# Two heads in one out projection: the halves of each head's outputs added by VectorE

## The chip, the cores and the metric

The kernel runs on one core of a Trainium2 chip. The metric is the device time of one execution in microseconds (us), and what counts is the median of several runs.

## What is computed

The program is one block of a network over 2048 rows of 128 channels: a mixture of eight experts, an RWKV layer, the mixture again, a small gated layer with integer weights, attention with 16 heads, and the gated layer again. The change is in the attention:

```python
xn = rms_norm(x, gamma)                       # 2048 x 128
q, k, v = split(xn @ w_qkv)                   # 16 heads of 64 columns
sim = einsum('bhid,bhjd->bhij', q * 64 ** -0.5, k)
attn = softmax(sim)
out = einsum('bhij,bhjd->bhid', attn, v)
x = x + concat_heads(out) @ w_out             # 1024 x 128
```

All of it is in float32. The kernel keeps this accuracy with products of a high and a low part: a value is rounded to the type that TensorE multiplies fast (high), what is left is a second number (low), and high x high, high x low and low x high are added.

## The kernel before

Channels lie on the partitions, rows on the free axis. The engines run programs of their own and meet at semaphores. In the attention stage every engine goes through the heads in order, two heads (even and odd) to a pair. A head has four chunks `c` of 512 queries, a chunk has eight groups `g` of two tiles of 128 keys. `main_chunk` stands once in the program of TensorE (line 930), of ScalarE (1258) and of VectorE (1619), with one `for g` loop each; `window` does it for GpSimd and for SyncE, which issues all DMAs. The order inside a group is written out by hand.

For each group TensorE forms transposed scores (`scores_t`, lines 879 and 880, four matmuls of 512 columns), then two matmuls of scores for the next head's maxima (`score_pair`, line 857), then the values of the group three before (`values`, PV_LAG = 3, lines 894 and 897). ScalarE makes exp twice, into `p_raw` (line 1253) and rounded into `p_h` (1256). GpSimd subtracts the two into `p_l` (line 608, four buffers: it waits until the values of four groups before are done). VectorE takes the maxima of the next head's scores (line 1580) and sums `p_raw` for the softmax's denominators: four pieces `first_half_sum` in groups 4 to 7 (line 1560), four pieces `whole_sum` in groups 0 to 3 of the next chunk (line 1574), each ahead of the group's maximum. `score_pair` waits for the maximum before it, since all of them use banks 4 and 5 of PSUM.

The values of a chunk gather in one bank of PSUM, 6 or 7 in turn. The weights of one values matmul hold the high and the low part of v side by side, so rows 0 to 63 of the bank become the sum with v's high part (p's high and low parts) and rows 64 to 127 the sum with v's low part. The two halves are not added: in group 2 of the next chunk (COPY_GROUP) ScalarE copies all 128 rows into `o_raw` (`copy_out`, line 1242), and the out projection adds them, because `w_o` holds the head's 64 rows of `w_out` twice (`load_o`, line 432).

The other of the two banks is the spare bank. The list SPARE says what TensorE does in it in which group: v and q, k projections for later heads, the turn of the maxima, the column sums of the denominators (line 906, group 4 or 5) and the out projection (line 913, group 7 or 6). The first of a chunk waits for `o_done`, since the bank held the sums of the chunk before; each later one waits until the one before it has been taken out (`evicted`).

The denominators go ScalarE, memory, VectorE, memory (`store_sums`, `load_sums`, `invert`, `store_inverse`, `load_inverse`) and come back two chunks later as `r_bc`, the reciprocals on all 128 partitions. GpSimd multiplies `o_raw` with it in group 3 (`scale`, line 631), TensorE projects, and VectorE adds the result to x in group 0 of the chunk after that, or in group 7 of the last (`add_out`, line 1598).

The last head has no next head, so no maxima, and it doesn't use the plan. For it TensorE spreads the sums over all partitions (`end_sums`, line 1008), VectorE inverts 512 columns out of PSUM (`end_invert`, 1605), multiplies `o_raw` (`end_scale`, 1612), TensorE projects (`end_out`, 1015) and VectorE adds (`end_add`, 1617); the plan for chunk c of it deals with chunk c - 1.

Of the kernel before, what the change touches and what calls it, by code (L numbers as in the profile page):

```python
# [5 lines left out]
fp32 = mybir.dt.float32  # L6
fp32r = mybir.dt.float32r
# [27 lines left out]
PV_LAG = 3  # L35
PRIME = 1
# [26 lines left out]
END_SUMS, END_INVERT, END_SCALE, END_OUT = 4, 5, 6, 7  # L63
END_TURN, END_LATE_OUT, END_LATE_ADD = 3, 5, 6
# [21 lines left out]
def macaron_kernel(nc, a, out, g_scratch, l_scratch, r_scratch):  # L86
    ctx = ExitStack()
    with ctx:
# [76 lines left out]
        p_l = sb("p_l", [128, 4, 2, CH], fp32r, two)  # L165
# [83 lines left out]
        end_l, end_r, end_o, end_ps = sem("end_l"), sem("end_r"), sem("end_o"), sem("end_ps")  # L249
# [42 lines left out]
        def spare_plan(head, c, par, project, has_next):  # L292

            plan = []
            for at, kind, n in SPARE[c]:
# [10 lines left out]
                if kind == "out" and not exists(before(head, c, 2)[0]):  # L306
                    continue
# [3 lines left out]
        def wait_x(eng, k, c):  # L311
# [5 lines left out]
            elif k == 1 or k == 3:  # L317
                eng.wait_ge(y_add, E * ((k // 2) * NC + c + 1))
            else:
                eng.wait_ge(x_ready, PRIME + NC * (k - 4) + c + 1)  # L320
# [13 lines left out]
        def _(sp):  # L334
# [58 lines left out]
            def store_sums(head, c):  # L393
                sp.wait_ge(l_done, chunk_of(head, c) + 1)
                sp.dma_start(l_scratch[ds(head, 1), chunk(c)], l_row[:, :]).then_inc(l_stored, 16)
# [36 lines left out]
            def load_o(head, par):  # L432

                for rows in (slice(0, DH), slice(DH, 128)):
                    sp.dma_start(w_o[par][rows, :], a["w_out"][ds(head * DH, DH), :]).then_inc(wo_loaded, 16)

            def window(pair, par, project, late_project, qk_after, v_after):
# [3 lines left out]
                for c in range(NC):  # L441
# [4 lines left out]
                    if exists(scaled[0]) and not (last and c > 0):  # L446
# [7 lines left out]
                    if c == 2 and not last:  # L454
# [6 lines left out]
                        if not (isinstance(head, int) and head == 0):  # L461
                            sp.wait_ge(out_ps, NC * head)
                        load_o(head + 1, 1 - par)
# [3 lines left out]
                    if exists(summed[0]) and not last:  # L467
# [10 lines left out]
            load_o(0, 0)  # L478
# [21 lines left out]
            window(PAIRS - 1, 1, False, False, False, False)  # L500
# [1239 lines left out]
```

## Time and profile before

| | us |
|---|---|
| median of three runs | 2123.63 |
| lowest and highest | 2120.82, 2125.29 |
| the profiled execution, whole | 2122.15 |
| its span in the trace | 2120.2 |
| attention from the first exp of head 0 to the last add | 600.5 to 2071.9 |

| engine | busy in the span |
|---|---|
| TensorE (PE) | 1998.7 us, 94% |
| VectorE (DVE) | 1773.6 us, 84% |
| GpSimd (POOL) | 1548.2 us, 73% |
| ScalarE (ACT) | 1458.5 us, 69% |

Matmuls are pipelined and overlap in the records, so a busy PE isn't PE at its peak. In a timeline, a number in brackets at the end of a row is the idle time of the engine ahead of it, with what ended that; a row without one followed the row ahead of it at once. `xn` is the tile that holds `o_raw` and `r_bc`.

### The profile page before, as it was taken

How to read it: one execution, taken by the hardware profiler on the slowest of the kernel's cores; microseconds unless marked ns; L12 is line 12 of the kernel's file. 1: busy time of each engine (PE TensorE's matmuls, PEld its weight loads, DVE VectorE, ACT ScalarE, POOL GpSimd, SP SyncE). 2: the span in 40 equal slices, each digit the busy share in tenths (PEclk: the TensorE clock that was granted, in tenths of full speed). 3: DMA queues.
4: the chain of work that ended last, by engine and by line, in shares of the span. 5: the costliest groups of instructions: out<-in, count | busy, mean ns of one | idle time of the engine just before them, and what ended most of it. 6: DMA issues, size and time to landing. Idle time of an engine off the chain costs nothing. (4 is left out here: it accounts for less than half of the span.)

```text
span 2120.2 us, 25547 instructions
## 1 busy us (share of the span) xinstructions
PE 1998.7 (94%) x8290; PEld 1423.8 (67%) x8290; DVE 1773.6 (84%) x1964; ACT 1458.5 (69%) x1800; POOL 1548.2 (73%) x767
## 2 busy tenths in 40 slices
PE   7999999998689999999999999999999999999867
PEld 5777777776457667666766766676676767666545
DVE  5677777655678998998999899899989989999885
ACT  4555455444257887887888787787878878787754
POOL 4332233232068999899899899999989999999862
PEclk9999999997789999999999999999999999999987
DMA  6111211300502230312213031231313213030000
GB/s 185 51 31 41 41 25 17 70 26 1 123 0 40 50 73 13 71 33 57 55 37 70 14 75 38 47 69 24 70 19 70 54 39 70 12 75 12 6 0 20
DMA packets 78942, 96.77 MB, mean 46 GB/s; under 512 B 32055, under 2 KB 35559, under 8 KB 78431
## 3 DMA queue, kind: packets, MB, share of 16 engines
q1 hardware_dynamic: 78814, 95.15, 20.5%
q8 instruction: 70, 1.15, 0.2%
q14 instruction: 58, 0.48, 0.1%
HBM read 43.19 MB, written 1.42 MB: 21 GB/s over the span
## 5 line engine op out<-in xcount | busy, mean ns | idle before, releaser
L608 POOL TENSOR_TENSOR p_l<-p_raw,p_h 128x1024 fp32r<-128x1024 f32 x512 | 1241.4, 2455 | 147.8 <-ACT p_h L1256 132.6
L1253 ACT ACTIVATE p_raw<-ps 128x1024 f32<-128x1024 f32 x512 | 567.2, 1108 | 242.8 <-PE ps L880 241.9
L1580 DVE TENSOR_REDUCE m_part<-ps 128x1 f32<-128x1024 f32 x480 | 584.5, 1218 | 125.7 <-PE ps L857 124.8
L1256 ACT ACTIVATE p_h<-ps 128x1024 fp32r<-128x1024 f32 x512 | 523.8, 1023 | 0.0
L879 PE MATMUL ps<-qa,ka 128*128 128x512 f32 x1024 | 445.8, 435 | 2.0 <-ACT m_t L1224 2.0
L880 PE MATMUL ps<-qb,kb 65*128 65x512 f32 x1024 | 409.2, 400 | 0.0
L894 PE MATMUL ps<-p_h,v_hl 128*128 128x512 f32 x1024 | 403.0, 394 | 1.0 <-POOL p_l L608 0.6
L1574 DVE TENSOR_REDUCE l_sum<-p_raw 128x128 f32<-128x1280 f32 x256 | 377.0, 1476 | 0.4
L857 PE MATMUL ps<-ka,qa 128*128 128x512 f32 x960 | 314.9, 409 | 11.9 <-DVE m_part L1580 11.8
L897 PE MATMUL ps<-p_l,v_hl 128*64 128x512 f32 x1024 | 321.6, 395 | 0.0
L1560 DVE TENSOR_REDUCE p_raw<-p_raw 128x128 f32<-128x1024 f32 x256 | 308.9, 1208 | 12.7 <-ACT p_raw L1253 12.7
L548 POOL TENSOR_TENSOR x<-x,y_gated 128x512 f32<-128x512 f32 x64 | 89.1, 1393 | 261.8 <-DVE y_gated L1448 261.7
L879 PEld LDWEIGHTS ps<-qa,ka 128*128 128x128 f32 x1024 | 195.1, 191 | 113.7 <-issue 73.3
L1439 DVE SCALAR_TENSOR_TENSOR h_l<-ps,h_h 128x512 fp32r<-128x512 f32 x256 | 176.0, 688 | 112.7 <-ACT h_h L1159 110.5
L1159 ACT ACTIVATE h_h<-ps 128x512 fp32r<-128x512 f32 x256 | 150.3, 594 | 168.5 <-PE ps L704 167.8
L894 PEld LDWEIGHTS ps<-p_h,v_hl 128*128 128x128 f32 x1024 | 193.7, 189 | 77.6 <-issue 3.3
L857 PEld LDWEIGHTS ps<-ka,qa 128*128 128x128 f32 x960 | 172.1, 190 | 90.6 <-DVE m_part L1580 57.6
L880 PEld LDWEIGHTS ps<-qb,kb 65*128 65x128 f32 x1024 | 195.2, 191 | 53.6 <-issue 16.4
L897 PEld LDWEIGHTS ps<-p_l,v_hl 128*64 128x64 f32 x1024 | 138.6, 135 | 71.7 <-issue 1.5
L702 PE MATMUL ps<-x_h,w_l 128*128 128x512 f32 x256 | 118.2, 462 | 4.6 <-DVE h_l L1439 2.5
L703 PE MATMUL ps<-x_h,w_h 128*128 128x512 f32 x256 | 102.5, 400 | 0.0
L704 PE MATMUL ps<-x_l,w_h 128*128 128x512 f32 x256 | 102.3, 400 | 0.0
(206 smaller groups left out, 2406.4 us busy)
## 6 DMA issues: line engine op xcount, KB each, us to landing
g_bc<-g_scratch SPq DMA_DIRECT2D x64, 256.0 KB, 5.2
xn<-r_scratch SPq DMA_DIRECT2D x59, 256.0 KB, 4.1
qa<-qk_hi SPq DMA_DIRECT2D x112, 128.0 KB, 2.4
ka<-qk_hi SPq DMA_DIRECT2D x56, 128.0 KB, 2.4
kb<-qk_hi SPq DMA_DIRECT2D x56, 128.0 KB, 2.4
ka<-xn SPq DMA_DIRECT2D x28, 128.0 KB, 2.3
qb<-xn SPq DMA_DIRECT2D x28, 128.0 KB, 2.3
ka<-qk_low SPq DMA_DIRECT2D x28, 128.0 KB, 3.7
```

Of the source, the lines that this page charges most:

```text
L608: nc.gpsimd.tensor_tensor(p_l[:, g % 4, :, :], slots(g), p_h[:, g % 4, :, :].bitcast(fp32), ALU.subtract).then_inc(pl_done, 1)
L857: last = mm(ps[:, 4 + b, :], qa[par][:, it * 128:it * 128 + 128], ka[par][:, chunk(2 * half + b)], start=True, stop=True)
L879: mm(st, ka[par][:, jt * 128:jt * 128 + 128], qa[par][:, ds(c * CH, CH)], start=True, stop=False)
L880: last = mm(st, kb[par][:, jt * 128:jt * 128 + 128], qb[par][:, ds(c * CH, CH)], start=False, stop=True)
L894: return mm(ps[:, bank, :], v_hl[:, par, 2 * g + j, :], p_h[:, g % 4, j, :], start=start, stop=stop)
L897: return mm(ps[0:DH, bank, :], v_hl[:, par, 2 * g + j, 0:DH], p_l[:, g % 4, j, :], start=False, stop=False)
L1253: af(slots(g), s_t, ACT.Exp).then_inc(raw_done, 1)
L1256: af(p_h[:, g % 4, :, :], s_t, ACT.Exp).then_inc(ph_done, 1)
L1439: stt(h_l[:, t % 4, :], ps[:, t % 4, :], 0.0, h_h[:, t % 4, :].bitcast(fp32), ALU.max, ALU.subtract).then_inc(h_done, 1)
L1560: nc.vector.tensor_reduce(p_raw[:, ACC, cols, 0], p_raw[:, 0:ACC, cols, :].rearrange("p g n b -> p n g b"), AX.XY, ALU.add).then_inc(half_ ...
L1574: nc.vector.tensor_reduce(l_sum[:, cols], p_raw[:, ACC:GROUPS + 1, cols, :].rearrange("p g n b -> p n g b"), AX.XY, ALU.add).then_inc(all_ ...
L1580: nc.vector.tensor_reduce(m_part[:, it, half:half + 1], ps[:, 4:6, :].rearrange("p b n -> p (b n)"), AX.X, ALU.max).then_inc(s_max, 1)
```

## The change

ScalarE now copies only the lower half, rows 64 to 127 of the sums, into `o_low[0:64]` (`move_low_half`, at the place of `copy_out`). VectorE adds this to rows 0 to 63 in PSUM and writes the result to `o_pair`, for an even head to rows 0 to 63 and for an odd one to rows 64 to 127 (`join_halves`, in group 3, behind the last piece of `whole_sum` and ahead of the group's maximum). `o_done` is given by this addition. `o_pair` takes the place of `xn` whole, 512 columns for each chunk; so `r_bc`, `qk_low` and `o_low` get memory of their own, for which `p_l` goes from four buffers to three.

One out projection of 128 rows then does a chunk for both heads of a pair, in the odd head's chunks and the two after them, and the add to x likewise: 32 of each instead of 64. `w_o` is loaded once per pair. The reciprocals go only to the head's 64 rows of `r_bc`. GpSimd scales 64 rows for an even head; for an odd one it takes all 128, and VectorE sets the other 64 rows of `r_bc` to one beforehand, once per odd head (`memset` in `invert`, which runs in group 0 of chunk 2).

The last head follows the common plan: sums through memory and GpSimd's `scale` for chunks 0 to 2, and only the last chunk goes by `end_sums`, `end_invert` and `end_scale`, on 64 rows. The last layer norm waits for `out_add`.

```diff
@@ tiles @@
-        p_l = sb("p_l", [128, 4, 2, CH], fp32r, two)
+        p_l = sb("p_l", [128, LOWS, 2, CH], fp32r, two)
-        l_row = sb("l_row", [1, CH], where=two)
-        qk_low2 = sb("qk_low2", [C, CH], where=two)
+        qk_low = [sb(f"qk_low{i}", [C, CH], where=two)[:, :] for i in range(2)]
+        r_bc = sb("r_bc", [128, CH], where=two)[:, :]
+        o_low = sb("o_low", [128, CH], where=two)
-        o_raw = xn[:, 0:2 * CH].rearrange("p (a n) -> p a n", a=2)
-        r_bc = xn[:, 2 * CH:3 * CH]
-        qk_low = [xn[:, 3 * CH:4 * CH], qk_low2[:, :]]
+        o_pair = xn.rearrange("p (a n) -> p a n", a=NC)
+        l_row = o_low[DH:DH + 1, :]
@@ which outs there are @@
+        def pair_done(head, c):
+            return head >= 0 and head % 2 == 1
+        def pair_chunk(head, c):
+            return NC * (head // 2) + c
+        def rows_of(par):
+            return slice(par * DH, par * DH + DH)
-                if kind == "out" and not exists(before(head, c, 2)[0]):
+                if kind == "out" and not pair_done(*before(head, c, 2)):
@@ SyncE @@
-                sp.dma_start(r_bc, r_scratch[ds(head, 1), chunk(c)].to_broadcast([128, CH])).then_inc(r_loaded, 16)
+                sp.dma_start(r_bc[rows_of(head % 2), :], r_scratch[ds(head, 1), chunk(c)].to_broadcast([DH, CH])).then_inc(r_loaded, 16)
-                for rows in (slice(0, DH), slice(DH, 128)):
-                    sp.dma_start(w_o[par][rows, :], a["w_out"][ds(head * DH, DH), :]).then_inc(wo_loaded, 16)
+                sp.dma_start(w_o[pair % 2][:, :], a["w_out"][ds(pair * 2 * DH, 2 * DH), :]).then_inc(wo_loaded, 16)
-                    if exists(scaled[0]) and not (last and c > 0):
+                    if exists(scaled[0]):
                         store_inverse(*scaled)
                         load_inverse(*scaled)
-                    if exists(summed[0]) and not last:
+                    if exists(summed[0]):
                         store_sums(*summed)
                         load_sums(*summed)
+            store_inverse(HEADS - 1, NC - 2)
+            load_inverse(HEADS - 1, NC - 2)
@@ GpSimd @@
-                if not (isinstance(n, int) and n < 4):
-                    pool.wait_ge(pv_done, n - 3)
-                nc.gpsimd.tensor_tensor(p_l[:, g % 4, :, :], slots(g), p_h[:, g % 4, :, :].bitcast(fp32),
+                if n >= LOWS:
+                    pool.wait_ge(pv_done, n - LOWS + 1)
+                nc.gpsimd.tensor_tensor(p_l[:, n % LOWS, :, :], slots(g), p_h[:, g % 4, :, :].bitcast(fp32),
                                         ALU.subtract).then_inc(pl_done, 1)
-                nc.gpsimd.tensor_tensor(o_raw[:, c % 2, :], o_raw[:, c % 2, :], r_bc, ALU.mult).then_inc(o_scaled, 1)
+                rows = slice(0, DH) if head % 2 == 0 else slice(0, 128)
+                if head % 2 == 1 and c == 0:
+                    pool.wait_ge(ones_set, head // 2 + 1)
+                nc.gpsimd.tensor_tensor(o_pair[rows, c, :], o_pair[rows, c, :], r_bc[rows, :], ALU.mult).then_inc(o_scaled, 1)
-                            if exists(scaled[0]) and not (last and c > 0):
+                            if exists(scaled[0]):
                                 scale(*scaled)
+                scale(HEADS - 1, NC - 2)
@@ TensorE @@
-                mm(ps[:, bank, :], w_o[par][:, :], o_raw[:, c % 2, :], start=True, stop=True).then_inc(out_ps, 1)
+                mm(ps[:, bank, :], w_o[pair % 2][:, :], o_pair[:, c, :], start=True, stop=True).then_inc(out_ps, 1)
-                plan = [] if last else spare_plan(head, c, par, project, has_next)
+                plan = spare_plan(head, c, par, project, has_next)
-                    if last:
...
-                        if g == END_OUT:
-                            pe.wait_ge(end_r, c + 1)
-                            end_out(c, spare)
-                end_sums(HEADS - 1, NC - 1, 4)
-                end_out(NC, 5)
+                end_sums(HEADS - 1, NC - 1, END_SUMS)
+                pe.wait_ge(out_add, NC * (PAIRS - 1) + NC - 2)
+                project_out(HEADS - 1, NC - 2, LATE_OUT)
+                end_out(END_OUT)
@@ ScalarE @@
-            def copy_out(head, c):
+            def move_low_half(head, c):
                 k = chunk_of(head, c)
                 act.wait_ge(pv_done, GROUPS * (k + 1))
...
-                af(o_raw[:, c % 2, :], ps[:, sums_bank(c), :], ACT.Copy).then_inc(o_done, 1)
+                if k > 0:
+                    act.wait_ge(o_done, k)
+                af(o_low[0:DH, :], ps[DH:128, sums_bank(c), :], ACT.Copy).then_inc(o_moved, 1)
@@ VectorE @@
+                if head % 2 == 1 and c == 0:
+                    nc.vector.memset(r_bc[0:DH, :], 1.0).then_inc(ones_set, 1)
                 nc.vector.reciprocal(r_col[:, c % 2, :], l_col[:, c % 2, :]).then_inc(r_ready, 1)
+            def join_halves(head, c):
+                k = chunk_of(head, c)
+                dve.wait_ge(o_moved, k + 1)
+                if head > 1:
+                    dve.wait_ge(out_ps, pair_chunk(head - 2, c) + 1)
+                tt(o_pair[rows_of(head % 2), c, :], o_low[0:DH, :], ps[0:DH, sums_bank(c), :], ALU.add).then_inc(o_done, 1)
                     elif exists(summed[0]):
                         whole_sum(*summed, g)
+                        if g == JOIN_GROUP:
+                            join_halves(*summed)
-                        if c > 0 and exists(added[0]) and not last:
+                        if c > 0 and pair_done(*added):
                             add_out(*added, spare_bank(c - 1))
-                    if (c, g) == (NC - 1, LAST_ADD) and not last:
+                    if (c, g) == (NC - 1, LAST_ADD) and par == 1:
                         add_out(head, c - 2, spare_bank(c))
-                    if last:
...
-                        if g == END_INVERT:
-                            end_invert(c, spare_bank(c))
-                        if g == END_SCALE:
-                            end_scale(c)
+                invert(HEADS - 1, NC - 2)
                 for i in range(PIECES):
                     whole_sum(HEADS - 1, NC - 1, i)
-                end_add(NC - 1, spare_bank(NC - 1))
-                end_invert(NC, 4)
-                end_scale(NC)
-                end_add(NC, 5)
+                join_halves(HEADS - 1, NC - 1)
+                end_invert(END_SUMS)
+                end_scale()
+                add_out(HEADS - 1, NC - 2, LATE_OUT)
+                add_out(HEADS - 1, NC - 1, END_OUT)
```

## Rows read from the trace of the kernel before

**Rows 1.** The windows view, by head: length, then busy time (instructions) of each engine.

```profile
core 0: us, PE busy (x) PEld busy (x) DVE busy (x) ACT busy (x) POOL busy (x), PEclk, DMA share, GB/s
...
1144.80:1238.70 93.90, 93.11 (x402) 65.73 (x401) 83.50 (x79) 74.37 (x85) 85.88 (x40) 1.00 0.22 47
1238.70:1327.60 88.90, 88.04 (x352) 59.82 (x351) 83.09 (x78) 71.96 (x81) 84.64 (x39) 1.00 0.23 51
...
1962.40:2056.60 94.20, 72.58 (x270) 48.68 (x268) 77.67 (x45) 63.97 (x69) 80.66 (x34) 0.91 0.02 4
```

**Rows 2.** Groups by form, whole span: count, busy us, mean ns, idle before, releaser.

```profile
L608 POOL TENSOR_TENSOR p_l<-p_raw,p_h 128x1024 fp32r<-128x1024 f32 x512 | 1241.4, 2455 | 147.8 <-ACT p_h L1256 132.6 <-issue 13.6
...
L1598 DVE SCALAR_TENSOR_TENSOR x<-ps,x 128x512 f32<-128x512 f32 x59 | 40.2, 681 | 0.0
...
L1506 DVE TENSOR_TENSOR x<-x,ps 128x512 f32<-128x512 f32 x4 | 2.7, 680 | 0.0
```

**Rows 3.** View of line 857: TensorE idle before it, us in total and times.

```profile
  DVE m_part L1580: 69.4, 159
```

**Rows 4.** Timeline of VectorE, head 6, chunk 1: start, length, line, out and in.

```profile
1173.86 1.22 DVE L1580 TENSOR_REDUCE m_part<-ps 128x1 f32<-128x1024 f32 x1
1174.99 1.48 DVE L1574 TENSOR_REDUCE l_sum<-p_raw 128x128 f32<-128x1280 f32 x1
1176.39 1.22 DVE L1580 TENSOR_REDUCE m_part<-ps 128x1 f32<-128x1024 f32 x1
...
1179.56 1.23 DVE L1580 TENSOR_REDUCE m_part<-ps 128x1 f32<-128x1024 f32 x1 [0.83 <-PE ps L857]
```

**Rows 5.** Timeline of TensorE, the same stretch: maxima's scores, values, first v matmul.

```profile
1175.13 0.73 PE L857 MATMUL ps<-ka,qa 128*128 128x512 f32 x2
1175.70 0.40 PE L894 MATMUL ps<-p_h,v_hl 128*128 128x512 f32 x1
...
1176.62 0.22 PE L843 MATMUL ps<-wv_hl,x_h 128*128 128x128 f32 x1
...
1178.89 0.63 PE L857 MATMUL ps<-ka,qa 128*128 128x512 f32 x2
```

**Rows 6.** Timeline of ScalarE, the same stretch: copy of the sums, p_h.

```profile
1174.59 0.59 ACT L1242 ACTIVATE xn<-ps 128x512 f32<-128x512 f32 x1
...
1176.23 1.02 ACT L1256 ACTIVATE p_h<-ps 128x1024 fp32r<-128x1024 f32 x1
```

**Rows 7.** Timeline of VectorE, head 7, where chunk 2 begins.

```profile
1283.69 0.68 DVE L1598 SCALAR_TENSOR_TENSOR x<-ps,x 128x512 f32<-128x512 f32 x1
1284.29 0.17 DVE L1594 RECIPROCAL r_col<-l_col 128x4 f32<-128x4 f32 x1
1284.38 1.20 DVE L1580 TENSOR_REDUCE m_part<-ps 128x1 f32<-128x1024 f32 x1
```

**Rows 8.** Timeline of ScalarE there: groups 0 and 1 of chunk 2.

```profile
1283.88 1.10 ACT L1253 ACTIVATE p_raw<-ps 128x1024 f32<-128x1024 f32 x1 [1.19 <-PE ps L880]
...
1286.22 1.11 ACT L1253 ACTIVATE p_raw<-ps 128x1024 f32<-128x1024 f32 x1 [0.35 <-PE ps L880]
```

**Rows 9.** Timeline of GpSimd, last head; the first row begins with head 14's last p_l.

```profile
1962.21 12.07 POOL L608 TENSOR_TENSOR p_l<-p_raw,p_h 128x1024 fp32r<-128x1024 f32 x5 [0.48 <-issue]
1974.24 1.26 POOL L631 TENSOR_TENSOR xn<-xn 128x512 f32<-128x512 f32 x1
...
1991.64 2.45 POOL L608 TENSOR_TENSOR p_l<-p_raw,p_h 128x1024 fp32r<-128x1024 f32 x1 [6.63 <-ACT p_h L1256]
...
2037.38 19.18 POOL L608 TENSOR_TENSOR p_l<-p_raw,p_h 128x1024 fp32r<-128x1024 f32 x8 [6.62 <-ACT p_h L1256]
```

**Rows 10.** Timeline of VectorE, last head: a multiplication, the last reciprocal, the last add.

```profile
2023.02 8.29 DVE L1612 TENSOR_TENSOR xn<-xn 128x512 f32<-128x512 f32 x1
...
2065.22 3.36 DVE L1605 RECIPROCAL xn<-ps 128x512 f32<-128x512 f32 x1 [0.62 <-PE ps L1008]
...
2071.19 0.69 DVE L1617 SCALAR_TENSOR_TENSOR x<-ps,x 128x512 f32<-128x512 f32 x1 [1.89 <-PE ps L1015]
```

More of the change, by code:

```diff
@@ L394, in store_sums @@
                 sp.wait_ge(l_done, chunk_of(head, c) + 1)
-                sp.dma_start(l_scratch[ds(head, 1), chunk(c)], l_row[:, :]).then_inc(l_stored, 16)
+                sp.dma_start(l_scratch[ds(head, 1), chunk(c)], l_row).then_inc(l_stored, 16)
             def load_sums(head, c):
@@ L460, in window @@
                             load_v(pair + 2)
-                        if not (isinstance(head, int) and head == 0):
-                            sp.wait_ge(out_ps, NC * head)
-                        load_o(head + 1, 1 - par)
+                        if par == 0 and pair < PAIRS - 1:
+                            if pair > 0:
+                                sp.wait_ge(out_ps, NC * pair)
+                            load_o(pair + 1)
                     if c == NC - 1 and project:
@@ L803, in mixtures, with quant_ffn @@
                     rwkv(t)
-            def quant_ffn(k, before):
+            def quant_ffn(k):
                 def gate_and_up(c):
@@ L816, in down @@
                 def down(c):
-                    pe.wait_ge(x_ready, PRIME + NC * (before - 3) + max(c - 1, 0))
+                    pe.wait_ge(x_ready, PRIME + NC * k + max(c - 1, 0))
                     for ht in range(HT1):
@@ L896, in low @@
                 def low(j):
-                    return mm(ps[0:DH, bank, :], v_hl[:, par, 2 * g + j, 0:DH], p_l[:, g % 4, j, :], start=False, stop=False)
+                    return mm(ps[0:DH, bank, :], v_hl[:, par, 2 * g + j, 0:DH], p_l[:, n % LOWS, j, :], start=False, stop=False)
                 high(0, g == 0, False)
@@ L922, in evicted @@
                 elif kind == "out":
-                    pe.wait_ge(out_add, k - 1)
+                    pe.wait_ge(out_add, pair_chunk(*before(head, c, 2)) + 1)
                 elif kind == "v":
@@ L943, in main_chunk @@
                             then = (head, pair, c - 1)
-                            previous = [] if last else spare_plan(head, c - 1, par, project, has_next)
+                            previous = spare_plan(head, c - 1, par, project, has_next)
                         else:
@@ L951, in main_chunk @@
                             evicted(*then, kind, n)
-                        if last and c > 0:
-                            pe.wait_ge(x_ready, PRIME + NC + c - 1) if c > 1 else pe.wait_ge(out_add, NC * (HEADS - 1))
                     if g >= PV_LAG:
@@ L1008, in end_sums, with end_out @@
                 mm(ps[:, bank, :], inv_c[:, :], l_sum[:, :], start=True, stop=True).then_inc(end_l, 1)
-            def end_out(i, bank):
-                pe.wait_ge(end_o, i + 1)
-                if i == 1:
-                    pe.wait_ge(wo_loaded, 32 * HEADS)
-                mm(ps[:, bank, :], w_o[0 if i == 0 else 1][:, :], o_raw[:, (i + 1) % 2, :], start=True, stop=True).then_inc(end_ps, 1)
+            def end_out(bank):
+                pe.wait_ge(end_o, 1)
+                mm(ps[:, bank, :], w_o[(PAIRS - 1) % 2][:, :], o_pair[:, NC - 1, :], start=True, stop=True).then_inc(out_ps, 1)
             def window(pair, par, has_next, project, late_project):
@@ L1260, in main_chunk @@
                 last = isinstance(head, int) and head == HEADS - 1
-                plan = [] if last else spare_plan(head, c, par, project, has_next)
+                plan = spare_plan(head, c, par, project, has_next)
                 summed = before(head, c, 1)
@@ L1279, in main_chunk @@
                             high_qk(head + 2, par, n, spare_bank(c), qk_hi, True)
-                    if last and (c, g) == (0, END_TURN):
-                        turn_maxima(head, 1, spare_bank(c))
                     if (c, g) == V_SPLIT[par] and (par == 0 or project):
@@ L1569, in whole_sum @@
                     dve.wait_ge(half_sum, PIECES * (k + 1))
-                    if isinstance(head, int) and head == HEADS - 1:
-                        dve.wait_ge(end_l, c + 1)
-                    elif not (isinstance(k, int) and k == 0):
+                    if k > 0:
                         dve.wait_ge(l_ps, k)
@@ L1634, in main_chunk @@
                         scaled, added = before(head, c, 2), before(head, c, 3)
-                        if c > 0 and exists(added[0]) and not last:
+                        if c > 0 and pair_done(*added):
                             add_out(*added, spare_bank(c - 1))
-                        if last and c > 0:
-                            end_add(c - 1, spare_bank(c - 1))
-                        if exists(scaled[0]) and not (last and c > 0):
+                        if exists(scaled[0]):
                             invert(*scaled)
```

85 lines of the change are left out of this document (34 added, 51 removed).

## The prediction

> **What bounds the kernel now.** I read the windows view first, with one stretch per head [rows 1]. An even head takes 93.9 us, an odd one 88.9, and in both TensorE is busy 99% of the time and VectorE 89 to 93%: two engines share the bound. The last head is another thing: it forms no maxima for a next head, TensorE is busy for only 72.6 of its 94.2 us, and the granted clock falls to 0.91 of full speed. So the heads in the middle and the last head get separate sums.
>
> The view by form gives the durations [rows 2]: p_l on GpSimd 2.45 us, an add out of PSUM on VectorE 0.68. Who waits for whom comes from the view of line 857, TensorE's scores for the maxima: TensorE stood 69.4 us for VectorE's maxima, in 159 places [rows 3]. Last come the timelines of one even chunk, pair 3's head 6, c = 1. On VectorE the maximum of group 2 starts at 1173.86 and ends at 1175.08, the row-sum piece of group 3 follows at 1174.99 and the maximum of group 3 at 1176.39, none with idle time before it; the first idle time, 0.83, is at group 4 [rows 4]. On TensorE the scores for group 3's maximum begin at 1175.13, 0.05 after the maximum before them ended [rows 5]. So **groups 0 to 3 run at VectorE's pace, groups 4 to 7 mostly at TensorE's**, and a delay of VectorE in group 3 reaches TensorE at group 4 almost whole.
>
> **The change, part by part: the join.** ScalarE's copy of the sums becomes a copy of their lower 64 rows; 512 columns either way, so its 0.59 us stay [rows 6]. VectorE gets a new addition in group 3 of each next chunk. Nothing like it stands in this stage; nearest is the tensor_tensor with one operand in PSUM, 0.68 us [rows 2], and in VectorE's queue an operation of this size moves the next one by 0.60 (1283.69 to 1284.29) [rows 7]. I take 0.60; the bounds are 0.60 and 0.68. It waits for the copy, which ended at 1175.18 [rows 6] while VectorE was in the sum piece until 1176.47 [rows 4], so the wait is covered by 1.3 us there. Queued behind the join is the maximum of group 3, and TensorE's next scores for maxima wait for that.
>
> **The bank.** TensorE's first use of the spare bank waits for the join instead of the copy. In four of a pair's eight chunks this use is a projection in group 3 (even c = 1, 2, 3, odd c = 3). In the rows it starts at 1176.62 [rows 5]; the join would run from 1176.39, where the maximum starts now [rows 4], to 1177.07, and with the 0.05 of a hand-over TensorE stands 0.50 us, with the scores of group 4 behind it. These four cost 0.50 each; VectorE's own 0.60 is then covered by its idle 0.83. In the other four the projection comes later, and VectorE's 0.60 itself reaches TensorE.
>
> **What goes.** Out projections and their adds happen for odd heads only. An add at group 0 is worth 0.60 on VectorE. An out projection costs 0.84: behind one ScalarE waits 1.19 for scores, in the next group 0.35 [rows 8]. VectorE had no idle time there either [rows 7], so where both go, 0.60 counts; where VectorE's add stood in group 7 behind TensorE (end of an even head), the 0.84 counts.
>
> **The memset.** Once per odd head, at c = 2, VectorE fills 64 rows with ones. No row shows this. Below, 0.09, the step of the small reciprocal [rows 7]; above, 8.29, the multiplication in the last head that ran beside GpSimd's p_l [rows 10]. I take 0.60, the step of a 512-column operation with one SBUF operand: the 8.29 us operation reads two SBUF operands, and the adds with one kept 0.68 beside the same p_l [rows 2, 7]. The Trainium skill (SBUF — State Buffer, Who interferes with whom) says a VectorE instruction with two SBUF inputs contends with a GpSimd one that reads SBUF, and one with at most one SBUF input outside the two-port modes doesn't; the 8.29 and the 0.68 agree.
>
> **The other half.** In odd heads the join writes partitions 64 to 127. VectorE's operations overlap by some 0.08 now (1284.29 starts before 1283.69 + 0.68 is over) [rows 7]; whether a switch of output rows loses that, before and after the join, no row shows. Bounds 0 and 7 x 0.08 = 0.56 an odd head (once at c = 3); I take the middle, 0.28.
>
> **At nothing:** one w_o load per pair instead of four, and half of the r_bc bytes, on queues that wait for others. Three p_l buffers instead of four: p_l of group n now needs the values of group n - 3, which TensorE has issued by 1176.62 [rows 5], while ScalarE's p_h, which p_l needs anyway, ends at 1177.24 [rows 6]. The cover is 0.5 us; without it every group would pay.
>
> **Sum of the middle.** Even head: 0.60 + 0.50 + 0.50 - 0.60 (add at c = 3) + 0.50 - 0.84 = 0.66. Odd head: c = 0 and c = 1 0.60 - 0.60 each, c = 2 0.60 + 0.60 (join and memset), c = 3 0.50, halves 0.28: 1.98. A pair: 2.64. Six pairs 15.8; pair 0 has no join at its first chunk, 2.0; head 14, without projections, 0.60 + 0.60 + 0.60 - 0.60 + 0.60 - 0.84 = 1.0. Together **+18.8 us**.
>
> **Sum of the last head.** Before, its scaling is on VectorE, 8.29 us at worst [rows 10]; TensorE waits for it, ScalarE gets no scores, and GpSimd stands 6.63 and 6.62 us [rows 9]. After, three of the four go to GpSimd and through memory, and GpSimd bounds this head alone: 32 p_l at 2.40 (19.18 for 8) and 4 scalings at 1.26 [rows 9] are 81.8. From the first p_l, 1962.21 + 2.41 = 1964.62, that ends at 2046.4; now it ends at 2056.56 [rows 9]: -10.2. A round trip through memory has more than a chunk, 20 us, to come back. The end: now 15.3 us from the last p_l to the last add (2071.88) [rows 9, 10]; after, the values 1.15 (0.92 of issue and the drain) [rows 5], copy 0.65 [rows 6], join 0.68, reciprocal 3.36, then the 3.30 from its end (2068.58) to the add's (2071.88) [rows 10]: 9.1, so -6.2. The row sums lie ahead of it then. Together **-16.4 us**; GpSimd's last scaling (1.25) lies under values, copy and join.
>
> **Net +2.4 us.** The profiled execution took 2122.15 us (span 2120.2 and 1.95 around it), so 2124.5; the median of the runs, 2123.63, lies 1.5 above it, so timed runs should show 2124.5 to 2126, and I say 2125.5. That is within 0.2% (4.2 us, about what a measurement of this kernel can tell from no change).
>
> **Rivals.** *(1) Slower: the memset is caught by GpSimd.* In odd heads at c = 2 p_l runs without a break, so the memset could stand like the multiplication did. At the four collided ones' worst row, 8.29, less my 0.60, seven times: +54, 2179; at one p_l, 2.45: +13, 2138.5. It decides as soon as a memset takes over about 1.5 us. Against it: it reads nothing. Chance 0.08.
> *(2) Slower: the switch of halves costs both overlaps.* Then 0.28 more in seven odd heads, +2.0: 2127.5, at the bound of 2127.9. It decides if VectorE's next start in those chunks lies behind the end of the join, not ahead of it. The Trainium skill (VectorE: DVE Perf Modes, Two Vector instructions with no wait between them) states it: an instruction whose output starts in another group of 32 partitions than the last is held until all before it have finished, and the next one back is held too. No run here shows it yet. Chance 0.24.
> *(3) Faster: the joins hide.* If TensorE's group 4 regains VectorE's 0.60 in the four chunks without an early projection, 2.4 a pair goes, some 17 in all: 2109. For it, VectorE's idle 0.83 at group 4 in the rows [rows 4]; against it, the 159 waits for the maxima [rows 3] and scores that start 0.05 behind them. Chance 0.14.
> *(4) The last head isn't freed:* the scalings through memory come late, or GpSimd waits for values with three buffers. Then up to 16.4 stays: 2142. Against it, the 20 us of room. Chance 0.06.
> The forecast: 0.48.
>
> **How the numbers follow.** Faster is rival 3's 0.14 and 0.04 of the forecast's 0.48, for a middle sum some 7 us smaller: 0.18. Slower is 0.08 + 0.06, half of rival 2's 0.24, and 0.08 of the forecast, for a middle sum some 3 us larger: 0.34. Within the bound lie 0.36 of the forecast and the other half of rival 2: 0.48. Range 2110 to 2138: it takes in rival 2 whole, rival 3 but for its far end, and stops at the low end of rival 1; some 0.18 stays outside.
>
> **What the profile after would show.** VectorE without idle time through group 3 and a join of about 0.68; TensorE standing 0.5 us before projections in group 3; an even head 0.7 longer, an odd one 2.0; a memset row near 0.6; joins of odd heads starting at or behind the end of the operation before; in the last head p_l without a break over some 82 us and no multiplication above 1 us. A longer memset, idle time of p_l on values, or heads that keep their length would prove this wrong.

## The result

The changed kernel is slower by half a per cent: ratio 1.0049 to the kernel before, 95% interval 1.0029 to 1.0068 (medians 2131.62 us of 11 runs and 2120.82 of 11). Its profiled execution took 2130.44 us, with a span of 2128.7; the span before was 2120.2. The time lies inside the range of the prediction, 6 us above its point, and on the other side of the 0.2% bound from the forecast.

Where the 8.4 us of span come from (before rounding), cut at the first exponential of attention, the first of the last head, and the end of the last p_l (the three stretches of each trace, in us):

```
                        before   after   difference   predicted
ahead of attention       600.5   598.3      -2.1          0
heads 0 to 14           1362.0  1387.2     +25.2       +18.8
last head, to its p_l     94.2    84.2      -9.9       -10.2
behind it                 63.7    58.9      -4.8        -6.2
```

The first row is no effect: nothing changes there, and in the nine experiments below the same stretch took between 597.3 and 602.9. Both predicted parts exist, with the predicted signs; the middle cost 6.4 us more than its sum, the end gave 1.7 less.

The windows view of after, by head, with the columns of [rows 1]:

```profile
core 0: us, PE busy (x) PEld busy (x) DVE busy (x) ACT busy (x) POOL busy (x), PEclk, DMA share, GB/s
1151.95:1246.77 94.82, 92.41 (x397) 64.48 (x396) 84.72 (x82) 75.37 (x85) 85.75 (x40) 1.00 0.19 41
1246.77:1337.77 91.00, 87.51 (x349) 58.90 (x348) 85.25 (x83) 73.02 (x81) 85.23 (x39) 1.00 0.19 43
1985.55:2069.76 84.21, 73.50 (x274) 44.36 (x272) 50.96 (x49) 67.82 (x73) 84.21 (x39) 0.99 0.05 9
```

Against [rows 1]: head 6 is 0.9 longer, head 7 2.1. TensorE has less to do in both (92.41 us, before 93.11; 87.51, before 88.04) and VectorE more (84.72, before 83.50; 85.25, before 83.09). In the last head GpSimd is busy for the whole of 84.21 us: it bounds it, as the sum had it. Groups of after by form, which answer to [rows 2], with the two new ones:

```profile
L1606 DVE TENSOR_TENSOR xn<-o_low,ps 64x512 f32<-64x512 f32 x64 | 43.2, 675 | 15.5 <-ACT o_low L1244 14.6
L1598 DVE SCALAR_TENSOR_TENSOR x<-ps,x 128x512 f32<-128x512 f32 x32 | 21.8, 682 | 5.7 <-PE ps L934 4.2 <-PE ps L1017 1.4
L1593 DVE MEMSET r_bc<- 64x512 f32 x8 | 3.9, 485 | 0.4
```

The join lasts 0.675 us (0.68 was taken), the memset 0.485 (0.60 was taken): neither *length* went wrong. And the view of TensorE's scores for the maxima (now line 878), which answers to [rows 3]:

```profile
  DVE m_part L1578: 127.4, 228
```

TensorE stood 69.4 us for VectorE's maxima, now 127.4. A new wait joins it, that for the join itself, ahead of qk and v projections; the join's view names who waits (us, times):

```profile
  PE ps L723: 5.5, 14
  PE ps L864: 4.3, 13
```

**A plain join**, in head 6, chunk 1, on VectorE, then on TensorE (timelines: start, length, line, out and in, idle before). They answer to [rows 4, 5]:

```profile
1182.92 1.48 DVE L1572 TENSOR_REDUCE l_sum<-p_raw 128x128 f32<-128x1280 f32 x1
1184.31 0.67 DVE L1606 TENSOR_TENSOR xn<-o_low,ps 64x512 f32<-64x512 f32 x1
1184.91 1.21 DVE L1578 TENSOR_REDUCE m_part<-ps 128x1 f32<-128x1024 f32 x1
1186.04 1.20 DVE L1560 TENSOR_REDUCE p_raw<-p_raw 128x128 f32<-128x1024 f32 x1
1188.08 1.22 DVE L1578 TENSOR_REDUCE m_part<-ps 128x1 f32<-128x1024 f32 x1 [0.84 <-PE ps L878]
```

```profile
1183.06 0.74 PE L878 MATMUL ps<-ka,qa 128*128 128x512 f32 x2
...
1185.04 0.33 PE L864 MATMUL ps<-wv_hl,x_h 128*128 128x128 f32 x1 [0.33 <-DVE xn L1606]
```

The join starts at 1184.31, before the sum piece has ended (1184.40), and moves the maximum by 0.60, as taken. The projection starts 1.98 us behind the maxima's scores; in [rows 5] it was 1.49. That is the 0.50 of the sum, to 0.01.

**A join of an odd head, and the memset**, in head 7, chunk 2:

```profile
1290.97 1.47 DVE L1572 TENSOR_REDUCE l_sum<-p_raw 128x128 f32<-128x1280 f32 x1
1292.49 0.48 DVE L1593 MEMSET r_bc<- 64x512 f32 x1
1292.90 0.11 DVE L1594 RECIPROCAL r_col<-l_col 128x4 f32<-128x4 f32 x1
...
1299.10 1.47 DVE L1572 TENSOR_REDUCE l_sum<-p_raw 128x128 f32<-128x1280 f32 x1
1300.59 0.68 DVE L1606 TENSOR_TENSOR xn<-o_low,ps 64x512 f32<-64x512 f32 x1
1301.31 1.22 DVE L1578 TENSOR_REDUCE m_part<-ps 128x1 f32<-128x1024 f32 x1
```

Here the join waits until the sum piece is over (1300.57) and starts at 1300.59, and the maximum starts 0.03 behind the join's end, not 0.07 ahead of it. Without a join the maximum would have started 0.08 before 1300.57, so it is 0.82 late instead of 0.60.

Chunk by chunk (first exponential of a chunk to that of the next, on ScalarE), in heads 10 and 13, chosen because no slow DMA issue (last section) falls into them in the kernels shown; c0 to c3 of each, and the sum of the eight, which stands for a pair:

```
                     head 10 (even)              head 13 (odd)               pair
before          22.57 24.86 23.42 22.91 |  22.55 22.37 20.92 22.84 |  182.44
after           23.38 25.47 23.17 22.83 |  22.29 22.59 22.49 23.56 |  185.78
e1_same_half    23.13 25.43 23.16 22.83 |  22.32 22.35 22.26 23.43 |  184.91
e2_no_ones      23.39 25.44 23.17 22.83 |  22.29 22.59 22.02 23.57 |  185.30
e3_last_memory  22.55 24.83 23.41 22.85 |  22.55 22.37 20.92 22.84 |  182.34
e4_three_low    22.55 24.84 23.41 22.87 |  22.55 22.37 20.93 22.87 |  182.37
e5_late_join    22.76 25.46 23.17 22.83 |  21.76 21.94 21.87 23.57 |  183.37
e6_more_late    22.76 25.43 23.09 24.35 |  22.02 21.95 21.86 23.56 |  185.00
e7_masked       22.69 25.44 23.09 24.34 |  22.03 21.91 21.33 23.52 |  184.34
e8_late_add     22.60 25.09 23.43 23.11 |  22.56 22.65 21.19 23.10 |  183.73
e9_pairs_best   22.69 25.44 23.16 22.83 |  21.80 21.88 21.35 23.76 |  182.91
```

This pair lost 3.34 us; the sum had 2.64.

**The last head**, on GpSimd, against [rows 9]:

```profile
1983.12 14.49 POOL L625 TENSOR_TENSOR p_l<-p_raw,p_h 128x1024 fp32r<-128x1024 f32 x6
1997.56 1.29 POOL L651 TENSOR_TENSOR xn<-xn,r_bc 64x512 f32<-64x512 f32 x1
1998.82 19.22 POOL L625 TENSOR_TENSOR p_l<-p_raw,p_h 128x1024 fp32r<-128x1024 f32 x8
```

p_l and scalings follow each other without a break, and the two gaps of 6.6 us are gone. **The tail**, on VectorE, against [rows 10], and the windows view of the stretch that the values of the last group lie in, of after and of the kernel without the fill (e2_no_ones, where the last p_l ends at 2065.60):

```profile
2072.61 0.68 DVE L1606 TENSOR_TENSOR xn<-o_low,ps 64x512 f32<-64x512 f32 x1 [3.36 <-ACT o_low L1244]
2073.70 3.36 DVE L1613 RECIPROCAL r_bc<-ps 64x512 f32<-64x512 f32 x1 [0.40 <-PE ps L1012]
...
2079.95 0.69 DVE L1598 SCALAR_TENSOR_TENSOR x<-ps,x 128x512 f32<-128x512 f32 x1 [1.45 <-PE ps L1017]
```

```profile
2066.00:2072.00 6.00, 4.44 (x11) 2.48 (x10) 3.25 (x3) 0.01 (x1) 4.99 (x3) 0.62 0.04 15
```

```profile
2062.00:2067.00 5.00, 2.55 (x10) 1.51 (x10) 3.05 (x3) 0.06 (x1) 4.85 (x3) 1.00 0.02 8
```

From the end of the last p_l (2069.76) the copy starts 2.2 us later, the reciprocal 3.9 and the last add ends after 10.9; 9.1 had been worked out. The granted clock is 0.62 of full speed there, a mean between the two levels, 1.2 and 2.4 GHz, after a head in which TensorE waited for GpSimd. In the other kernel, whose last head lacks the fill alone, it stood at 1.00 in that stretch, and the last add ended 9.6 us behind the last p_l; no run shows why.

### The profile page after: what moved, and what is told of

It reads as the page before. It is cut to its first block, busy times and chain, and to the rows that moved or that the text cites. A ratio compares the mean times of both kernels' runs of the same rounds, so it can differ in the third digit from the quotient of the medians.

```text
span 2128.7 us, 25496 instructions
## 1 busy us (share of the span) xinstructions
PE 1985.6 (93%) x8226; PEld 1400.1 (66%) x8226; DVE 1763.8 (83%) x2000; ACT 1475.5 (69%) x1804; POOL 1555.4 (73%) x771
## 4 chain that ended last, share of the span: by engine, by line
PE 48%; DVE 34%; issue 10%; POOL 4%; ACT 2%; DMA 1%; SPq 1%; DVEq 0%; ACTq 0%; POOLq 0%
DVE m_part L1578 12%; DVE l_sum L1572 12%; PE ps L878 6%; PE ps L900 5%; PE ps L723 5%; PE ps L725 5%; PE ps L724 5%; PE ps L901 4%; PE ps L915 4%; PE ps L918 4%; PE ps L927 3%; POOL p_l L625 3%; DVE p_raw L1560 2%; DVE m_part L1666 1%; DVE xn L1606 1%
## 5 line engine op out<-in xcount | busy, mean ns | idle before, releaser
L900 PE MATMUL ps<-qa,ka 128*128 128x512 f32 x1024 | 430.1, 420 | 2.0 <-ACT m_t L1228 2.0
```

Of the source, the lines that this page charges most:

```text
L900: mm(st, ka[par][:, jt * 128:jt * 128 + 128], qa[par][:, ds(c * CH, CH)], start=True, stop=False)
```

## Experiments

Two theories stood then. **A**: the middle's excess is the switch of output rows, whose price was bounded too low; the sum's other terms hold. **B**: it is the place, since VectorE and TensorE take turns in these chunks, so that any work of VectorE counts at more than its length. The first four kernels tell them apart and take the parts one by one.

**e1_same_half.** Odd heads' joins write the same partitions as those of even heads:

```
-                tt(o_pair[rows_of(head % 2), c, :], o_low[0:DH, :], ...
+                tt(o_pair[0:DH, c, :], o_low[0:DH, :], ...
```

> The changed kernel with the joins of odd heads written to partitions 0 to 63 like those of even heads (so the odd heads' result is not where the out projection reads it; all instructions and their sizes stay). Theory A, the switch of output rows costs both overlaps: joins of odd heads then start 0.08 us before the operation ahead of them ends, like those of even heads, the step from that end to the next operation's start goes from 0.74 to 0.51 us, the first chunk of an even head and the last three of an odd one are 0.22 us shorter each, and 30 joins x 0.23 = 6.9 us go in all: 2131.6 becomes about 2125, a ratio to the kernel before of 1.0015 to 1.002. Theory B, the 0.22 comes from another thing at those places (the copy by ScalarE that ends late, or the place in the odd head): the step stays at 0.74 and the time at 2131.6.

Measured: 2123.15 us, ratio 1.0009 (0.9996 to 1.0022), against 1.0049 of the changed kernel. VectorE in head 7, chunk 2:

```profile
1296.49 1.47 DVE L1572 TENSOR_REDUCE l_sum<-p_raw 128x128 f32<-128x1280 f32 x1
1297.88 0.67 DVE L1606 TENSOR_TENSOR xn<-o_low,ps 64x512 f32<-64x512 f32 x1
1298.48 1.21 DVE L1578 TENSOR_REDUCE m_part<-ps 128x1 f32<-128x1024 f32 x1
```

The step is 0.60 again, with no other edit than the output's rows. In the chunks: 0.25 less in c0 of the even head, 0.24, 0.23 and 0.13 in c1 to c3 of the odd one, 0.87 a pair. Theory A; a late copy or the place in the odd head, which B had for the 0.22, is out. Seven pairs make some 6 us of the 8.5 between the medians. Others lie where no join of the middle stands: in the profiled executions the stretch behind the last p_l takes 56.9 us instead of 58.9, and the one ahead of attention 1.0 less.

**e2_no_ones.** The fill is left out, and GpSimd's wait for it:

```
-                if head % 2 == 1 and c == 0:
-                    nc.vector.memset(r_bc[0:DH, :], 1.0).then_inc(ones_set, 1)
```

> The changed kernel without the fill of 64 rows with ones (rows 0 to 63 are then multiplied by old inverses). Theory A: VectorE is the bound at that place, so chunk 2 of each odd head is shorter by what the fill moves the next operation, 0.5 us, and the kernel by 8 x 0.5 = 4 us: about 2127.5, ratio 1.003. Theory B: VectorE's idle time later in the chunk absorbs it, and the heads keep their lengths: 2131.6.

Measured: 2128.63, ratio 1.0031 (1.0018 to 1.0044). Chunk 2 of the odd head is 0.47 shorter, no other chunk of the shown pair moves. The fill costs 0.5 where it stands, and nothing takes it up.

**e3_last_memory.** The kernel before, with the last head's part of the change alone. The edit is that part of the diff; its core:

```
-                plan = [] if last else spare_plan(head, c, par, project, has_next)
+                plan = spare_plan(head, c, par, project, has_next)
...
-                            if exists(scaled[0]) and not (last and c > 0):
+                            if exists(scaled[0]):
                                 scale(*scaled)
```

> The kernel before with one part of the change alone: the last head's row sums go through memory as those of the others do, its scalings to GpSimd; ScalarE still copies 128 rows and each head has its own out projections. Theory A, the two parts of the change are independent: the middle heads keep the lengths of before (93.7 and 88.8 us), the last head shortens by 9.9 us up to its last p_l as in the changed kernel, and the tail behind it by 4.4 to 5.5 us, since no join stands there: 14.3 to 15.5 us less than before, about 2106, ratio 0.993. Theory B, the last head gains because its out projections are halved or its joins free the bank earlier: then less than 8 us are gained here, ratio over 0.996.

Measured: 2106.61 us, ratio **0.9929** (0.9913 to 0.9945): faster than both kernels. Its three stretches from the first exponential on:

```profile
600.72:1962.38 1361.66, 1348.43 (x5585) 935.39 (x5585) 1240.13 (x1158) 1094.31 (x1228) 1273.89 (x574) 1.00 0.22 46
1962.38:2046.41 84.03, 73.72 (x278) 44.88 (x276) 49.18 (x46) 66.67 (x73) 84.03 (x38) 1.00 0.10 17
2046.41:2103.70 57.29, 44.31 (x154) 29.54 (x154) 32.27 (x48) 22.25 (x39) 16.32 (x14) 0.77 0.05 19
```

The middle is that of before (1361.97), the last head takes 84.03 us instead of 94.2, and what is behind it 57.3 instead of 63.7: 5.4 less up to the last add, as A had it, and 1.0 less behind that, which A hadn't. The two parts of the change are independent, and the whole gain belongs to this one.

**e5_late_join.** The join in group 5 instead of 3 where the spare bank isn't used before:

```
-                        if g == JOIN_GROUP:
-                            join_halves(*summed)
+                    if exists(summed[0]) and g == (LATE_JOIN if c == 0 or (par == 1 and c < NC - 1) else JOIN_GROUP):
+                        join_halves(*summed)
```

with LATE_JOIN = 5; in c0 of all heads the turn is in group 5 and the column sums in 6, in c1 of odd heads the column sums in 5 and the turn in 6.

> The changed kernel with the join at group 5 instead of 3 in the chunks whose spare bank isn't needed in group 3 (chunk 0 of every head, chunks 1 and 2 of odd heads), and the turn and column sums there one group later where they came before group 5. Theory A, groups 0 to 3 are VectorE's and groups 4 to 7 TensorE's: VectorE's idle time of 0.8 to 0.9 us at group 5 takes the join, and the four chunks lose their 0.80, 0.60, 0.83 and 0.82 us: some 3 us a pair, 20 to 22 in all, about 2110, ratio 0.995. Theory B, VectorE bounds these chunks throughout: the delay only moves, and the time stays within 5 us of 2131.6.

Measured: 2112.24 us, ratio 0.9955 (0.9938 to 0.9971), 19 us less than the changed kernel. The four chunks are shorter by 0.62, 0.53, 0.65 and 0.62: 2.4 a pair, four fifths of what A said. VectorE in head 7, c1:

```profile
1275.09 1.21 DVE L1561 TENSOR_REDUCE p_raw<-p_raw 128x128 f32<-128x1024 f32 x1
1276.33 0.68 DVE L1607 TENSOR_TENSOR xn<-o_low,ps 64x512 f32<-64x512 f32 x1
1277.04 0.16 DVE L1585 TENSOR_REDUCE m_col<-m_part 128x4 f32<-128x8 f32 x1
1277.12 1.22 DVE L1579 TENSOR_REDUCE m_part<-ps 128x1 f32<-128x1024 f32 x1
```

In the changed kernel VectorE had 0.84 us of idle time ahead of that last maximum; here the join fills it. Of B, that VectorE's time counts wherever it stands in these chunks, this leaves a fifth.

**e4_three_low.** The kernel before, p_l with three buffers instead of four, which the sum had at nothing:

> The kernel before with three p_l buffers instead of four, nothing else. Theory A: p_l waits for ScalarE's p_h anyway, which ends 0.5 us after the values that free a third buffer, so the heads keep the lengths of before (93.7 and 88.8 us) and the time stays at 2122, ratio 1.000 within 0.002. Theory B: GpSimd waits for values in places where it runs without a break; then TensorE waits for p_l, as the 11 us of idle time before the first values matmul in the changed kernel suggest, and up to 11 us are lost: ratio up to 1.005.

Measured: 2119.28, ratio 0.9992 (0.9978 to 1.0006), and the chunks of the middle keep their lengths (the shown pair to 0.04 us; a few, like chunk 0 of head 6, are longer by a slow DMA issue). The 11 us that values of after stood for p_l belong to the last head, where GpSimd is the bound. In the middle of after GpSimd does wait 1 us for values once a pair, but TensorE stands only 0.3 us in all for p_l there: the cover was enough.

**e6_more_late.** The same shift for c2 and c3 of even heads: join in group 4, first use of the bank in 4:

```
+             (0, 2): ((4, "v", 2), (5, "sums", 0), (6, "v", 3)),
+             (0, 3): ((4, "qk", 0), (5, "sums", 0), (6, "qk", 1), (7, "qk", 2))}
...
-LOW_QK = {(3, 4): 0, (3, 6): 1}
+LOW_QK = ({(3, 5): 0, (3, 7): 1}, {(3, 4): 0, (3, 6): 1})
```

> The kernel with late joins (2112.2 us), and in chunks 2 and 3 of even heads the join at group 4 too, with the first use of the spare bank moved from group 3 to group 4 (v, column sums and qk each one group later, and the second qk's low part with them). Theory A, what costs 0.60 there is that VectorE has no idle time ahead of the next scores in group 4, since TensorE's extra work of 0.84 comes at the end of group 3: with that work at the end of group 4, the join lies under it, and both chunks lose 0.6 us, 14 joins x 0.6 = 8 us: about 2104. Theory B, VectorE's 0.60 counts wherever it is put in these chunks, as VectorE is their bound: 2112 as with late joins alone.

Measured: 2128.71, ratio 1.0038 (1.0025 to 1.0051), 16 us worse than e5_late_join. A fell here: c2 is 0.08 shorter, and c3 is 1.52 longer. VectorE in head 6, c2:

```profile
1213.61 1.21 DVE L1564 TENSOR_REDUCE p_raw<-p_raw 128x128 f32<-128x1024 f32 x1
1214.74 0.67 DVE L1610 TENSOR_TENSOR xn<-o_low,ps 64x512 f32<-64x512 f32 x1
1215.33 1.21 DVE L1582 TENSOR_REDUCE m_part<-ps 128x1 f32<-128x1024 f32 x1
1216.46 1.21 DVE L1564 TENSOR_REDUCE p_raw<-p_raw 128x128 f32<-128x1024 f32 x1
1218.51 1.23 DVE L1582 TENSOR_REDUCE m_part<-ps 128x1 f32<-128x1024 f32 x1 [0.84 <-PE ps L882]
```

The idle time moved to group 5 with the projection, and the join stands one group ahead of it, as it did before the shift. Idle time of VectorE lies *behind* extra work of TensorE, and a join that frees the bank for the chunk's first extra work lies ahead of it. The 1.52 of c3 is another thing. ScalarE in head 10, at the end of c3:

```profile
1624.42 0.69 ACT L1211 ACTIVATE qk_hi<-ps,qk_scale 128x512 fp32r<-128x512 f32 x1 [2.00 <-DMA kb<-qk_hi]
1625.00 1.07 ACT L1259 ACTIVATE p_raw<-ps 128x1024 f32<-128x1024 f32 x1
```

Its copy of the third qk waits 2.00 us for the moves of the second, which now start a group later, and the next chunk's first exponential stands behind it. In the other even heads of the middle up to 12 this wait is 2.01 to 2.04, in head 6, with a slow DMA issue, 4.14; in e5_late_join the copy has 0.11 us of idle time ahead of it. With c0 behind it this makes 1.6 a pair, some 11 of the 16 us; the profiled execution has slow DMA issues in heads 3, 6 and 8 besides.

**e7_masked.** On e6_more_late, two edits more. ScalarE copies one half of the sums to the rows where the result belongs; in odd heads one operation then adds over all rows, a column of zeros and ones keeping rows 0 to 63; the ones are filled once:

```
+                if head % 2 == 0:
+                    tt(o_pair[0:DH, c, :], o_pair[0:DH, c, :], ps[0:DH, sums_bank(c), :], ALU.add)
+                else:
+                    stt(o_pair[:, c, :], ps[:, sums_bank(c), :], mask[:, 0:1], o_pair[:, c, :], ALU.mult, ALU.add)
```

> The kernel of the run before this one, and two edits more: odd heads' sums are added by one operation over all 128 rows, ScalarE copying the high half to the rows of the result first and a column of zeros and ones keeping rows 0 to 63, so that its output starts at partition 0; and the ones are filled once instead of eight times, the even heads' inverses having rows of their own. Theory A, the switch of rows costs 0.22 us at a join that VectorE bounds, which after the late joins is the one in chunk 3 of odd heads alone, 0.13 us by the run with joins in the same half, and the fill 0.49 in chunk 2: 0.6 us a pair, 4 to 5 us in all, about 2100 if the run before gives 2104. Theory B, the wider operation waits for GpSimd's scaling or for ScalarE's copy into the result: idle time before it, and no gain.

Measured: 2126.81, ratio 1.0029 (1.0014 to 1.0044); the intervals of this run and the last overlap. In the chunks, 0.53 went in c2 of the odd head, as A had it, and 0.04 in c3, where A had 0.13. All odd heads' joins of the middle start ahead of the end of the operation before them. So the switch can be avoided without giving up the pairing: the operation takes 0.744 us instead of 0.68, but the next one starts 0.57 us behind the end of the one ahead, not 0.74.

**e8_late_add.** On e3_last_memory, out projections in group 6 and their adds in group 7 of the same chunk, in five chunks of a pair:

```
-                    if (c, g) == (NC - 1, LAST_ADD):
-                        add_out(head, c - 2, spare_bank(c))
+                    if g == LAST_ADD and (par, c) != (0, 1) and exists(before(head, c, 2)[0]):
+                        add_out(*before(head, c, 2), spare_bank(c))
```

> The kernel before with the last head's sums through memory (2106.6 us), and the out projections of five of a pair's chunks in group 6 instead of 7, their adds by VectorE in group 7 of the same chunk instead of group 0 of the next. Theory A: group 0 belongs to VectorE's stretch, where an add counts 0.60; behind an out projection TensorE is 0.84 late and VectorE idle, so the add in the group after it is covered: 0.6 us in 5 chunks of a pair, 3 a pair, 20 in all, about 2087, ratio 0.984. Theory B: VectorE bounds these chunks as a whole, or GpSimd's scaling isn't done by group 6: the 0.6 counts in group 7 too, and the time stays at 2106 or rises.

Measured: 2115.97, ratio 0.9984 (0.9970 to 0.9997), 9 us worse than e3_last_memory. A fell: the five chunks whose group 0 lost its add are 0.26 to 0.28 longer, and the ones that took it into group 7 keep their lengths to 0.05 where they lost none. VectorE at the end of head 7, c1, and the start of c2:

```profile
1284.99 0.68 DVE L1582 SCALAR_TENSOR_TENSOR x<-ps,x 128x512 f32<-128x512 f32 x1
1285.92 1.23 DVE L1564 TENSOR_REDUCE m_part<-ps 128x1 f32<-128x1024 f32 x1 [0.25 <-PE ps L864]
```

Behind the add VectorE now stands 0.25 us. In [rows 7] the add at group 0 had no idle time on either side: as I read it, it stood behind the out projection of group 7 and already filled the gap that this left. What an add is worth can't be told from the group's number; extra work of TensorE just ahead of it counts too.

**e9_pairs_best.** On e5_late_join, the two edits of e7_masked, and the add of odd heads' chunk 0 in group 7 of c2, behind its projection in group 6:

> The changed kernel with late joins in chunk 0 of all and chunks 1 and 2 of odd heads (2112.2 us), odd heads' sums added over all 128 rows with a column of zeros and ones, the ones filled once, and the add of odd heads' chunk 0 in group 7 of chunk 2, behind its out projection in group 6. Theory A: 0.53 us in chunk 2 of an odd head for the fill and 0.05 in chunk 3, as the run with both showed, 0.6 more for the add: 1.2 a pair, some 8 in all: 2104. Theory B, the add counts in group 7 as it did in group 0: 4 in all, 2108.

Measured: 2112.36, ratio 0.9961 (0.9946 to 0.9977), no different from e5_late_join. In the shown pair, 0.52 went in c2, but c3, whose group 0 lost its add, is 0.19 longer, like such chunks in e8_late_add. The pair is at 182.91 us against 182.34 of e3_last_memory. Pairing the out projections can be brought to about the cost of not pairing them, but no version here brought it below; the fastest kernel is **e3_last_memory**.

## Why the prediction was right or wrong

**The bound** was read rightly: in groups 0 to 3 a join's whole step reached TensorE (0.81 in c0 of head 10, 0.61 in c1), and rival 3, joins that hide, did not happen. Where joins were moved to VectorE's idle time they did hide, by four fifths.

**The join's step**: 0.60 taken, 0.60 measured in even heads. **The bank**: 0.50 taken; TensorE starts the projection 0.49 later, but c1 of the even heads, where nothing else changes, grew by 0.56 to 0.61. The rest is in the projection: from its first matmul to the next scores it took 1.39 us behind the idle stretch, in heads 2 to 12, and 1.29 before. For the three chunks of an even head: +0.28.

**The other half** is the step that failed. Rival 2 had the mechanism, and the forecast took half of it; but its price, 0.08 for each overlap, came from the overlap alone. Measured, the join starts 0.03 *after* the end ahead of it, and the next operation 0.03 after the join: 0.11 on either side, 0.22 a join, four joins a pair. The sum of these joins was 0.60 x 3 + 0.50 + 0.28 = 2.58; they cost 0.82, 0.83, 0.82 and 0.73 = 3.20, +0.62 a pair. And I counted seven overlaps as an upper bound of 0.56, where 0.88 was to be had: the bound of rival 2 was not a bound. The Trainium skill (VectorE: DVE Perf Modes, Two Vector instructions with no wait between them) names among the instructions that are held until all before them have finished those whose output starts in another group of 32 partitions than the last, and so the next one back; the trace agrees for all 28 joins of the odd heads 1 to 13, which start 0.03 us after the end ahead of them. In e1_same_half, by the rows alone, and in e7_masked they start some 0.08 before it.

**The memset**: 0.60 taken, 0.5 measured by leaving it out. Rival 1 fell: each of the eight took 0.485 us, and each ran beside a p_l. The number of SBUF operands was the right thing to look at here (8.29 with two in [rows 10], 0.485 with none).

**What goes**: 2.64 taken. In the shown pair the eight joins make 5.6 (0.60 each, and 0.2 more or, at odd c3, 0.1 for the switch) and the memset 0.5; it lost 3.34, so what goes gave 2.7. The total is right, the places aren't: 0.85 went in c2 of the even head and in c0 of the odd one, which ended in an out projection, and some 0.6 in the chunk behind each; but c2 of the odd head, whose group 0 lost its add too, is 0.25 longer than join and memset make it. A pair's sum thus becomes 2.64 + 0.28 + 0.62 - 0.11 = 3.43, where the shown pair measured 3.34. For six pairs that is 20, with pair 0 (1.9) and head 14 (0.8) 22.8 of the 25.2 measured. Most of the rest, 2.2 us, is two slow DMA issues in heads 8 and 11 (below), for which the sum had no term.

**The last head**: -10.2 predicted, -9.9 measured, and -10.1 alone in e3_last_memory; the round trips had room, and rival 4 fell. **The tail**: -6.2 predicted and -4.4 measured up to the last add. Values and column sums were taken at the clock of the middle (values 1.15 us); at the lower level the values took 2.2, and the reciprocal waited 0.40 for the column sums, which the sum had ahead of it. **Nothing** for three p_l buffers: right, by e4_three_low. For w_o and r_bc no run takes the term apart.

So the net was +2.4 because a cost of the middle 6.4 too small and a gain of the end 1.7 too large erred to the same side. That the time is still inside the range is in part luck: the range reached up to 2138 for rival 1, which did not happen, and rival 2 at its stated price ended at 2127.5. With the measured price of 0.22 a join it would have stood at 2130.

## What to carry to other kernels

Where an engine bounds a stretch, look at each added operation's place in its queue, not at its length alone: an output that started at another partition than its neighbours' cost a third of the join's step here, and what stands just ahead of it on the other engine helped to decide whether it counted at all. A change of several parts should be summed, and tried, part by part: here one part alone gave 15 us, and the other cost 25. An operation that frees a bank or a buffer has to run before the next user of it; idle time that comes from this user lies behind the operation and can't cover it.

## What the runs showed that was not expected

**A memset waits too.** All eight fills start 0.05 us after the end of the operation ahead, though they and their neighbours all begin at partition 0; the operation behind them overlaps by 0.07, near the usual 0.08. The waits ahead of the fill aren't the reason: in the other chunks the same waits stand ahead of the reciprocal, and it overlaps by 0.08. No run shows why.

**A DMA issue can take three times as long, and not at random places.** SyncE's issue of a move takes 0.60 us. In heads 0 to 14 of each kernel here, five to ten of its issues took over 0.35 us more than is usual for their line, 2.2 us at most. Where one falls among the moves at the start of a head, ScalarE's next copy waits for its source and VectorE behind it. SyncE in heads 8 and 6 of after (two issues in one row), then ScalarE in head 8:

```profile
1337.54 2.33 SPq L431 DMA_DIRECT2D qa<-qk_hi  x2
```

```profile
1151.72 1.10 SPq L431 DMA_DIRECT2D qa<-qk_hi  x2
```

```profile
1343.00 0.69 ACT L1207 ACTIVATE qk_hi<-ps,qk_scale 128x512 fp32r<-128x512 f32 x1 [1.35 <-DMA kb<-qk_hi]
```

Chunk 0 of head 8 is 1.1 us longer for it, and head 11's likewise. The places recur. Seven kernels here, after among them, issue the same moves; in six of them one of the moves at the start of head 8 is slow, and chunk 0 there is 0.9 to 1.2 us longer. In before and the three kernels made from it, none is slow there; the same two other issues, in heads 10 and 11, are slow in three of these four. So it isn't chance alone which issue is slow; what it depends on, no run shows. A comparison of undisturbed heads is safer than one of whole spans: where nothing is changed, their chunks agree to some 0.06 us from kernel to kernel.
